# Four of sixteen states get their scan input from spread rows of B, in a new order of pieces

## What is computed

```python
xz = x @ in_proj_w.T
xc, z = split(xz, 2)                      # 256 channels each
u  = conv1d(xc, conv_w, 4 taps, causal) + conv_b
dt = clip(sigmoid(u @ dt_w.T + dt_b), 1e-4, 1.0)
A  = -exp(A_log)                          # 256 channels x 16 states
B, C = u @ B_w.T, u @ C_w.T               # per token, 16 states each
def step(state, (ut, dtt, bt, ct)):       # over the 256 tokens of a sequence
    dA = exp(clip(dtt[:, :, None] * A, -5, 5))
    dB = dtt[:, :, None] * bt[:, None, :] * ut[:, :, None]
    state = dA * state + dB + 1e-6
    y = sum(state * ct[:, None, :], -1) + D * ut
y = y * silu(z);  x = x + y @ out_w.T
```

## Time and profile before

| | |
|---|---|
| time, median of three runs | 1420.82 us (1420.7 to 1425.83) |
| the profiled execution | 1425.94 us, span 1424.1 us |
| TensorE matmul, weight load | 1233.5 us (87%), 1033.9 us (73%) |
| VectorE | 1177.5 us (83%) |
| ScalarE | 899.6 us (63%) |
| GpSimd | 845.9 us (59%) |
| granted TensorE clock, mean | 0.963 of full speed |
| DMA | 132.28 MB, 93 GB/s over the span |

### The profile page before, as it was taken

One profiled execution on the slowest core, in us unless ns is written; L12 is line 12 of the kernel. 1 busy time (PEld: TensorE's weight loads), 2 busy tenths in 40 slices (PEclk: granted clock), 3 DMA queues, 4 the chain that ended last, 5 costly groups with the idle time before them and its releaser, 6 DMA issues.

```text
span 1424.1 us, 27089 instructions
## 1 busy us (share of the span) xinstructions
PE 1233.5 (87%) x8709; PEld 1033.9 (73%) x8709; DVE 1177.5 (83%) x2236; ACT 899.6 (63%) x1450; POOL 845.9 (59%) x1354
## 2 busy tenths in 40 slices
PE   5788888888989898998989898998989899897884
PEld 3566766677777777787777777787777778786773
DVE  0499999988898979998898979988898979897322
ACT  2775756567577767677676767677676767761221
POOL 3435553754557773867657773867657773665344
PEclk9699999999999999999999999999999999999897
DMA  5000000032323242243313242243312233266672
GB/s 175 1 1 8 1 9 1 27 115 65 115 59 95 84 138 80 67 128 98 119 58 95 84 134 83 67 128 94 122 58 86 93 124 103 79 193 204 201 242 80
DMA packets 110653, 132.28 MB, mean 93 GB/s; under 512 B 10032, under 2 KB 81584, under 8 KB 110384
## 3 DMA queue, kind: packets, MB, share of 16 engines
q1 hardware_dynamic: 102320, 113.73, 25.7%
q0 software_dynamic: 8192, 16.79, 4.0%
HBM read 102.37 MB, written 28.11 MB: 92 GB/s over the span
## 4 chain that ended last, share of the span: by engine, by line
PE 40%; DVE 28%; issue 13%; ACT 10%; POOL 6%; DMA 2%; SPq 1%; DVEq 0%; POOLq 0%; ACTq 0%
DVE h L1201 12%; DVE yT L1219 11%; PE p_hT L1000 7%; PE p_db L983 6%; PE p_misc L1032 5%; PE p_dn L1146 5%; PE p_gu L1134 3%; PE p_gu L1125 3%; PE p_misc L1043 3%; POOL xs_dram L740 2%; ACT L931 2%; ACT dA L835 2%; ACT hm L931 2%; PE p_misc L1026 2%; PE p_misc L1069 1%
## 5 line engine op out<-in xcount | busy, mean ns | idle before, releaser
L1201 DVE TENSOR_TENSOR_SCAN h<-dA,p_db 128x512 f32<-128x512 f32 x512 | 602.5, 1204 | 74.7 <-PE p_db L983 46.5
L698 POOL TENSOR_SCALAR dBT<-wT,bcT 128x256 f32<-128x256 f32 x704 | 339.3, 482 | 346.8 <-ACT wT L865 139.4
L1219 DVE SCALAR_TENSOR_TENSOR yT<-p_hT,bcT,yT 128x256 f32<-128x256 f32 x960 | 402.7, 471 | 31.0 <-PE p_hT L1000 30.9
L983 PE MATMUL p_db<-ident,dBT 128*128 128x128 f32 x2048 | 300.6, 280 | 58.3 <-DVE h L1201 52.0
L835 ACT ACTIVATE dA<-dt_sb,A_sb 128x510 f32<-128x510 f32 x512 | 332.8, 711 | 28.4 <-DVE h L1201 27.2
L983 PEld LDWEIGHTS p_db<-ident,dBT 128*128 128x128 f32 x2048 | 239.7, 144 | 107.4 <-issue 95.8
L1000 PE MATMUL p_hT<-ident,h 128*128 128x128 f32 x2048 | 292.2, 282 | 25.9 <-DVE yT L1219 17.0
L1000 PEld LDWEIGHTS p_hT<-ident,h 128*128 128x128 f32 x2048 | 239.1, 145 | 66.5 <-DVE yT L1219 30.8
L740 POOL DMA_INDIRECT xs_dram<-xn,slot x128 | 127.1, 993 | 69.6 <-issue 33.9
L891 ACT ACTIVATE dBT<-wT,eps,bcT 128x256 f32<-128x256 f32 x320 | 163.9, 592 | 0.1
L754 POOL DMA_INDIRECT ysel<-ys_dram,slot x128 | 123.5, 965 | 65.2 <-issue 32.6
(11 more groups left out here) (153 smaller groups left out, 1478.3 us busy)
## 6 DMA issues: line engine op xcount, KB each, us to landing
wring<-w_moe_dram SPq DMA_DIRECT2D x177, 384.0 KB, 4.3
xt<-xs_dram SPq DMA_DIRECT2D x41, 256.0 KB, 5.0
ys_dram<-yo SPq DMA_DIRECT2D x41, 256.0 KB, 2.3
dA<-w_moe_dram SPq DMA_DIRECT2D x14, 384.0 KB, 4.8
x_sb<-x_dram SPq DMA_DIRECT2D x16, 256.0 KB, 4.3
out_dram<-x SPq DMA_DIRECT2D x16, 256.0 KB, 2.4
xs_dram<-ysel SPq DMA_DIRECT2D x4, 512.0 KB, 5.8
xs_dram<-xn,slot POOLq DMA_INDIRECT x128, 2.3
```

The lines of the kernel that those rows point to most:

```text
L698: op = pool.tensor_scalar(dBT[:, j % DBT_RING, c], wT[:, g % 2, c], bcT[:, g % 2, c, n:n + 1], STATE_EPS, ALU.mult, ALU.add)
L983: mm = pe.transpose(p_db[half][:, c * P:(c + 1) * P], dBT[:, j % DBT_RING, c, half * P:(half + 1) * P], ident[:])
L1201: dve.tensor_tensor_scan(h[:, j % 2, half], dA[:, j % DA_RING, half], p_db[half][:], 0.0, ALU.mult, ALU.add).then_inc(scan_done, 1)
L1219: op = dve.scalar_tensor_tensor(yT[:, g % 2, cc], p_hT[pair][:, c], bcT[:, g % 2, cc, NS + n:NS + n + 1], yT[:, g % 2, cc], ALU.mult, ALU.add)
```

## The change

Four of the sixteen states are of a new kind "d": `KINDS` becomes "psdsdsdsdpppppps", seven p, five s, four d. For them nothing is made by token and TensorE does not turn anything into p_db. Once a group a new piece "br" transposes the 16 columns of B of each chunk (from bcT) into p_misc, ScalarE empties it into bc_sb (16x512), and SyncE stores that to DRAM ("R"). For each d unit SyncE loads one row of it, spread over all 128 partitions, into the ring brow ("b", 7 units ahead). GpSimd multiplies w_sb (w by channel, 128x1024) by that row, one instruction into the ring dBs; ScalarE adds epsilon to it in place ("e", one instruction of 128x1024); and the scan of a d unit reads dBs in SBUF instead of p_db in PSUM.

The dBT ring has two places instead of three, the xn2T ring three instead of four, the decays run three units ahead instead of four, and weights and tiles are loaded four and six slots ahead of their quad instead of two and five. The order of pieces of every engine within a group is new; the orders after the last group stay. The core of the diff:

```diff
-KINDS = "pppsspspppppppss"
+KINDS = "psdsdsdsdpppppps"
-DBT_RING = 3
+DBT_RING = 2
+DBS_RING = 2
+ROW_RING = 2
+ROW_LEAD = 7
+EPS_LEAD = 2
-EXP_LEAD = 4
+EXP_LEAD = 3
+XN2T_RING = 3
-WEIGHT_LEAD = 2
+WEIGHT_LEAD = 4
-LOAD_LEAD = 5
+LOAD_LEAD = 6
 POOL_SLOTS = (
-    "", "d d c c S d c c C C ln1", "", "d C c d gate0 gate1 c C S S", "d C S S", "C c ln2 c C d d d C S", "",
-    "c c c c S d clip S C S d C d C S", "", "", "c c w0 w1 C S d S", "C", "", "c d S C c d S", "",
-    "d C C S S")
+    "c c", "d d c S c ln1 C d d", "", "C d c gate0 c S C C gate1 S d", "S ln2 S", "c c C C C d d d c c S c d",
+    "", "c S S C S clip d C C w0 d w1 C S c c", "", "", "S C d", "C c S", "", "S c d", "", "C d C C S S d S")
 SP_SLOTS = (
+    "", "b b T T W xl W W Y W O b Y b Y", "", "", "O T Y b O W T Y T Y Y", "Y T b O W T O W", "",
+    "b b O b O T W T O T", "", "Y W b Y Y O b", "", "R O T O W W b O T Y Y W b W T b Y", "", "",
+    "b O W O W T W Y", "O O b T T Y")
...
+            def store_rows(g):
+                sp.wait_ge(misc_emptied, misc_at["br", g])
...
+                sp.dma_start(bc_rows[g % 2], bc_sb[:]).then_inc(rows_stored, 16)
+            def load_row(j):
...
+                if n == KINDS.index("d"):
+                    sp.wait_ge(rows_stored, 16 * (g + 1))
+                at_least(sp, dbs_by_pool, at - ROW_RING + 1)
+                sp.dma_start(brow[:, at % ROW_RING], bc_rows[g % 2, n:n + 1].broadcast_to([P, TOK])
+                             ).then_inc(row_loaded[at % ROW_RING], 16)
...
             def state_input(j):          # GpSimd
+                if KINDS[n] == "d":
+                    at = of_kind("d", j)
+                    pool.wait_ge(row_loaded[at % ROW_RING], 16 * (at // ROW_RING + 1))
+                    at_least(pool, scan_done, 2 * unit_of("d", at - DBS_RING) + 2 if at >= DBS_RING else 0)
+                    pool.tensor_tensor(dBs[:, at % DBS_RING], w_sb[:], brow[:, at % ROW_RING].rearrange(
+                        "p (o t) -> p o t", o=1).broadcast_to([P, HALVES, TOK]), ALU.mult).then_inc(dbs_by_pool, 1)
...
+            def add_eps(j):              # ScalarE
+                at = of_kind("d", j)
+                act.wait_ge(dbs_by_pool, at + 1)
+                act.activation(dBs[:, at % DBS_RING], dBs[:, at % DBS_RING], ACT.Identity, bias=eps[:]
+                               ).then_inc(dbs_ready, 1)
...
             def inputs_by_channel(j, half):
+                if kind == "d":
+                    return
...
             def scan_state(j, half):
-                dve.wait_ge(db_by_pe, 2 * j + half + 1)
-                dve.tensor_tensor_scan(h[:, j % 2, half], dA[:, j % DA_RING, half], p_db[half][:], 0.0,
+                if KINDS[j % NS] == "d":
+                    at = of_kind("d", j)
+                    dve.wait_ge(dbs_ready, at + 1)
+                    source = dBs[:, at % DBS_RING, half]
+                else:
+                    dve.wait_ge(db_by_pe, 2 * by_token(j) + half + 1)
+                    source = p_db[half][:]
+                dve.tensor_tensor_scan(h[:, j % 2, half], dA[:, j % DA_RING, half], source, 0.0,
                                        ALU.mult, ALU.add).then_inc(scan_done, 1)
```

More of the change, by code:

```diff
@@ L343, in of_kind, with unit_of, by_token @@
     return full * KINDS.count(kind) + KINDS[:n].count(kind)
+def unit_of(kind, at):
+    full, n = divmod(at, KINDS.count(kind))
+    return NS * full + [m for m in range(NS) if KINDS[m] == kind][n]
+def by_token(j):
+    return j - of_kind("d", j)
 def build(nc, x, w_in, w_z, w_conv, w_dt, w_bc, w_out, chan, w_router, b_router,
-          w_shared, w_moe, xs0, xs1, ys0, ys1, out):
+          w_shared, w_moe, bc_rows, xs0, xs1, ys0, ys1, out):
     xs, ys = (xs0, xs1), (ys0, ys1)
@@ L414, in build @@
         xn2 = sb("xn2", [P, 4, CHUNKS, DM])
-        xn2T = sb("xn2T", [P, 4, TOK])
+        xn2T = sb("xn2T", [P, XN2T_RING, TOK])
         stage = dA[:].rearrange("p n h t -> p (n h t)")
@@ L503, in build @@
         db_by_pe = sem("db_by_pe")
+        rows_stored = sem("rows_stored")
+        row_loaded = [sem(f"row_loaded{j}") for j in range(ROW_RING)]
+        dbs_by_pool = sem("dbs_by_pool")
+        dbs_ready = sem("dbs_ready")
         exp_done = sem("exp_done")
@@ L611, in _ @@
                         load_x(k)
+                    if name == "R" and group_of(k, 1) is not None:
+                        store_rows(k + 1)
+                    if name == "b":
+                        load_row(u + ROW_LEAD)
                     if name == "T":
@@ L861, in empty_misc @@
                         "p (c n) -> p c n", c=CHUNKS), ACT.Copy).then_inc(misc_emptied, 1)
+                if name == "br":
+                    at_least(act, rows_stored, 16 * g)
+                    act.activation(bc_sb[:], p_misc[0:NS, :], ACT.Copy).then_inc(misc_emptied, 1)
                 if name in ("wT0", "wT1"):
@@ L868, in empty_misc @@
                 if name == "xn2T":
-                    at_least(act, up_in_psum, 2 * QUAD["shared", g - 4] + 2 if g >= 4 else 0)
-                    act.activation(xn2T[:, g % 4], p_misc[:], ACT.Copy).then_inc(misc_emptied, 1)
+                    at_least(act, up_in_psum, 2 * QUAD["shared", g - XN2T_RING] + 2 if g >= XN2T_RING else 0)
+                    act.activation(xn2T[:, g % XN2T_RING], p_misc[:], ACT.Copy).then_inc(misc_emptied, 1)
             def empty_xt(b, q):
@@ L944, in _ @@
                         decays(u + EXP_LEAD)
+                    if name == "e":
+                        add_eps(u + EPS_LEAD)
                     if name == "d":
@@ L979, in inputs_by_channel @@
                 kind = KINDS[j % NS]
+                if kind == "d":
+                    return
+                turned = by_token(j)
+                before = max([m for m in range(max(0, j - NS), j) if KINDS[m % NS] != "d"], default=-1)
                 pe.wait_ge(dbt_by_pool if kind == "p" else dbt_by_act, of_kind(kind, j) + 1)
-                at_least(pe, scan_done, 2 * (j - 1) + half + 1)
+                at_least(pe, scan_done, 2 * before + half + 1)
                 for c in range(CHUNKS):
                     mm = pe.transpose(p_db[half][:, c * P:(c + 1) * P],
-                                      dBT[:, j % DBT_RING, c, half * P:(half + 1) * P], ident[:])
+                                      dBT[:, turned % DBT_RING, c, half * P:(half + 1) * P], ident[:])
                 mm.then_inc(db_by_pe, 1)
@@ L1048, in use_misc @@
                         mm = pe.matmul(p_misc[:, c * EXPERTS:(c + 1) * EXPERTS],
-                                       xn2T[:, g % 4, c * P:(c + 1) * P], wr_sb[:], start=True, stop=True)
+                                       xn2T[:, g % XN2T_RING, c * P:(c + 1) * P], wr_sb[:], start=True, stop=True)
                 if name == "rank":
@@ L1071, in use_misc @@
                                            start=q == 0, stop=q == HALVES - 1)
+                if name == "br":
+                    pe.wait_ge(misc_emptied, misc_at["bc", g])
+                    for c in range(CHUNKS):
+                        mm = pe.transpose(p_misc[0:NS, c * P:(c + 1) * P], bcT[:, g % 2, c, 0:NS], ident[:])
                 if name in ("z0", "z1"):
```

37 lines of the change are left out of this document (28 added, 9 removed), and 43 rows, old and new, of tables (ACT_FIRST, ACT_SLOTS, DVE_SLOTS, PE_FIRST).

## The result

The changed kernel takes 1457.0 us in the median of four runs (1455.06 to 1459.75), the kernel before beside it 1420.76 us (1418.25 to 1425.83): a ratio of 1.026, 95% interval 1.023 to 1.029. It is slower, by 36 us where +10 was forecast: the direction and the range hold, the size is three and a half times the forecast. The kernel before alone takes 1419 to 1421 us on some of these chips and 1470 to 1483 on others; 1.026 is from a chip of the first kind, 1.022 from one of the second.

What follows compares the result with a forecast made beforehand. TensorE and VectorE, both at 90% in later groups, wait for each other; VectorE bounds three early groups. TensorE -18, shared interface +29, the rest 0: +11 us, 1437 on the profiled execution, scaled to 1431; range 1388 to 1462.

Steps and rivals of the forecast that it cites:

- the share of the lock that reaches the end: VectorE's 43 us of waiting on the shared SBUF read interface: 8 us count early, 21 later; GpSimd held counted 0.
- What bounds: Later groups: TensorE and VectorE, both at 90%, wait for each other; three early groups are VectorE's, 68 us instead of 65.7.
- TensorE, -18 us: Fewer transposes into p_db take 1.5 us a group off the chain, 18 us over twelve groups; bounds 0 and 37.
- The scan and the lock, +29 us: 128 scans with two SBUF inputs wait for GpSimd's reading instructions: 2.7 us a group, +29 reaching the end.
- not for descriptor work: A VectorE instruction with two SBUF tensors waits for GpSimd's reading instruction but not for indirect DMA's descriptor work.
- GpSimd's product, 1.90 us: Four 128x1024 products a group, 1.90 us each, 7.6 us, replace 7.7 us of small instructions; GpSimd's load stays.
- Rings and order, 0 within 12: Shorter rings cost small slack; the new order's value can't be read from any row: 0, within 12 us either way.
- ScalarE's addition: Adding epsilon over 128x1024 takes 1.15 us per d unit, hidden in ScalarE's idle time: 0 to +10 us.
- SyncE and the rows: Row stores and loads through DRAM stay hidden by the long lead: 0, bound +10 us; at the start 0 to +3.
- B: Rival: faster, VectorE's waits fall into gaps or the scan doesn't hold the interface; some 1395 us, chance 0.35.
- C: Rival: slower, GpSimd held by scans delays products or gates, then ScalarE's addition and the scan; 1463 us, chance 0.11.
- A: The forecast itself: TensorE's gain is there, the shared read interface takes more; 1431 us, range 1424 to 1445, chance 0.38.

Runs made afterwards that it cites:

- the run in which the d scans wait: Changed kernel, TensorE again turning eight tiles into p_db per d unit; d scans still read SBUF but wait for them: 1.038 of the kernel before.
- the dummy transposes: Changed kernel, TensorE again making eight transposes per d unit into p_db, which nothing reads or waits for: 1.026 of the kernel before.

## Why the prediction was wrong in size

Two steps of the sum failed. The first is the share of the lock that reaches the end: I let six tenths of VectorE's lengthening through behind the early groups and counted GpSimd's side at 0, +29 in all, where the lock measures +35 to +43. The second is the rest, forecast as -18 for TensorE and 0 for everything else: with the lock taken away it measures 0.996 to 1.001, -6 to +1 us. The paragraphs below take the terms one by one.

**What bounds.** Two engines at 90% waiting for each other: right. The first three groups are VectorE's: one of them took 67.5 us for 65.7, against 68 forecast. But I had let all of the lock's 8 us in these three groups count, and they lost 1.8 us together; up to the sixth bcT nothing is lost at all (381.4 us in both kernels). By the run with all scans on p_db the lock costs some 4 us up to there, and the rest of the change gives as much back.

**TensorE, -18 us.** The number is close, the reason isn't. From the run in which the d scans wait to the changed kernel it is 1.2%, 17 us. But by the prediction's step it was TensorE's time on the chain, and in the changed kernel the load alone measured nothing (1.026 with 64 more matmuls a pair). In the kernel before, transposes that the scans wait for did count, 10 us. The forecast "TensorE busy 139 to 140 us in a pair" failed: 147.8, for 145.8 with 58 matmuls more. The granted clock goes with it. Two stretches of 5 us in the pair 713.6 to 881 of the changed kernel (columns as in rows 2):

```profile
733.60:738.60 5.00, 4.48 (x26) 4.49 (x27) 4.93 (x12) 2.18 (x4) 0.00 (x0) 0.66 0.00 2
753.60:758.60 5.00, 4.90 (x28) 4.69 (x28) 3.64 (x6) 4.29 (x10) 4.63 (x9) 0.66 0.07 23
```

1.0 is TensorE's upper level, 2.4 GHz, and 0.5 its lower, 1.2 GHz, so at 0.66 it ran at the lower one for most of the stretch; five such stretches lie in that pair, one in the like pair of before. Ahead of the one at 733.6 TensorE had waited 2.27 us for VectorE. With the dummy transposes the whole run's clock is 0.961, without them 0.941 (0.963 before). The lighter load isn't enough for the lower clock, though. The kernel with all scans on p_db and the ring of three has as many matmuls as the changed kernel, and its clock is 0.960 (engine totals as rows 1):

```profile
PE 1192.5 (84%) x8261; PEld 989.7 (70%) x8261; DVE 1173.9 (83%) x2236; ACT 976.6 (69%) x1532; POOL 872.7 (61%) x1162
```

There TensorE's busy time did fall, from 1233.5 to 1192.5 us; with the lock in place it is 1214.8. Since the time didn't follow the clock (1.026 with and without the dummy transposes), the clock shows in the busy time and not in the slowdown.

**The scan and the lock, +29 us.** The mechanism was right and told by the right rows: mean 1.51 us for a forecast 1.53, single ones of 3.4 us. A held scan doesn't end with GpSimd's instruction, as the small products of the earlier trace rows did, but about its own length later. 128 x (1513 - 1204) ns is 39.6 us for 43. The step that failed is the share that reaches the end: 35 to 43 us did, not 29, and nearly all of it behind the early groups, where I had counted 21. Beside VectorE's own lengthening the lock holds GpSimd: it is busy 121.7 us a pair against 111.4 with all scans on p_db, and I had counted this at 0. That it can cost is shown by the kernel before with four SBUF scans: scans 1.23 us, GpSimd's products 51 ns longer each, 1.5% slower. My "not for descriptor work" was read from one side only: at 1285.99 VectorE wasn't held by an indirect DMA, but an indirect DMA behind a scan is held (1.73 us at 769.41).

**GpSimd's product, 1.90 us.** It takes 2.37 us. The row of 1898 ns has its spread operand along the innermost axis, and the new one repeats whole rows; that costs nearly what two plain halves do (2 x 1.274 us is 2.55). That the axis makes the difference is argued, not tested. The 2.1 us that I had estimated from the Trainium skill's cycles for an element ("GPSIMD Engine Reference", section 2.1) was nearer, if still too low. By itself the length costs nothing measurable; half of it was worth 2.2% through the lock.

**Rings and order, 0 within 12; product and addition, 0.** This is the other half of the second failed step. With the d units' relief undone and no lock, the new order with its product and addition stands at 1.032, some 46 us over the kernel before. I called the order zero because no row shows it. The working then reads +46 (order, product, addition, with transposes and waits), -52 (transposes and waits gone, short scans), +43 (lock): 37 us. With 1.001 for 0.996 the last two are -44 and +35. The 46 us are no pure price of the order: it was made without these transposes, and in it VectorE waits 71.4 us for p_db (62.5 for them and 8.9 for the others) where the kernel before waits 46.5. How the 46 us divide isn't settled. The order without d units (short rings with it) cost 9%, the short ring in the old order 5.6%, yet without the lock neither the ring nor half a product was worth anything measurable; ScalarE's addition was never taken out by itself. The sign of the forecast came out right and its size didn't; that gains and losses beside the lock nearly cancel (-6 to +1 us) was in no term of it.

**ScalarE's addition** takes 1.144 us (1.15 forecast). **SyncE and the rows:** no wait of TensorE for wring appears; a row lands in 3.7 us. Counted at nothing, and none of it is seen in the chain (SPq 1%).

**The rivals.** B, faster, would have needed a scan that doesn't take the lock; but even with the lock gone the kernel stood at 0.995 to 1.001, where B said 0.98. C has the right place (GpSimd held) and the period (163 to 168 us for the forecast "over 164"), but not the chain of waits: the scans don't wait for the addition of epsilon (0.8 us in all). The truth is A's mechanism with C's other half of the lock.

## What to carry to other kernels

When a VectorE instruction gets a second SBUF operand beside a busy GpSimd, price both sides: VectorE's lengthening, and GpSimd's, indirect DMAs included; and price it for the state after the change, since the same lock cost 0.6 to 1.5% while the scans still waited for TensorE, and 2.5 to 3.0% when they didn't. Ask of a relief whether it takes away load or a dependency: in the changed kernel eight transposes that nobody waits for cost nothing, and the scan's wait for them 1.2%. And a new hand-made order is not zero because no row shows it; without the d units it was made for, this one cost 9% with its short rings.

## What the runs showed of the hardware

A scan with two SBUF inputs and a GpSimd instruction that reads SBUF exclude each other: up to 3.45 us for a scan of 1.2, ended in all 46 long cases 1.07 to 1.09 us after GpSimd's instruction. Such a scan holds an indirect DMA that begins during it, too: up to 1.99 us for 0.97. A GpSimd product of 128x1024 takes 2.37 us in one, 2 x 1.27 in two, 4 x 0.73 in four, so a fixed part of some 0.18 us seems to ride on each (0.73 doubled less 1.27, an estimate). In two it was the cheapest for the whole kernel at 1.3% over the kernel before; no version that leaves nothing out came under the kernel before.
